# Three-pass query and output projections, and attention copies dealt out anew over ACT and DVE

## The chip, the cores and the metric

The kernel runs on one NeuronCore of a Trainium2 chip. It has five engines with a queue each, which meet only at semaphores: TensorE (PE, matmuls), VectorE (DVE), ScalarE (ACT), GpSimd (POOL) and SyncE (SP, which here issues DMAs). The metric is the device time of one execution in microseconds, lower being better.

## The reference

A gated cross-attention block with a mixture-of-experts feed-forward behind it, all in float32:

```python
# x: (4, 1024, 256), context: (4, 77, 256), 16 heads of 16
q = layernorm(x) @ w_q + b_q;  k = ctx @ w_k + b_k;  v = ctx @ w_v + b_v
attn = softmax(where(mask == 0, -10000, q k^T / 4))          # 1024 x 77 a head
x = x + tanh(g_x) * ((attn v) @ w_o + b_o)
xn = layernorm(x)
routed = top-2 of 4 experts, each silu(xn eg^T) * (xn eu^T) @ ed^T, width 688
shared = silu(xn sg^T) * (xn su^T) @ sd^T
out = x + tanh(g_f) * (routed + shared)
```

## The kernel before

The 4096 rows are cut into 16 units of 256 rows. The first third of the program is a software pipeline of 18 steps, numbered `i` from 0. In step `i` unit `i` has its scores and exponentials; unit `i-1` has its probabilities transposed (`prob_T`, five groups through the one bank `p_t`, each copied to `pT` by `t_copy`) and multiplied by the values (`prob_v`); unit `i-2` has its output projection (`out_proj`), second layernorm (`stats_2`, `rstd2`, `normed_2`), transpose and router logits; unit `i+1` has its transpose (`x_T`) and query projection (`q_T`). From step 4 (`FIRST`) on, the shared expert of earlier units fills TensorE: `gate_up(n, c)` for six chunks `c` of width 128 and `down(n)`. Chunks 0 and 1 and the `down` of the unit before stand in an even step, chunks 2 to 5 in an odd one. After the last step the rest of the shared expert runs along with the routing and the experts' weights, and then come 67 tiles of routed rows. The change touches neither of these later stages.

The order in each engine's queue is written out by hand: a function `step(i)` for each engine calls the pieces in turn. An engine takes its queue strictly in order, so a piece that waits holds all behind it.

Each unit's probabilities come in four quarters `j`: 64 query-by-head blocks of scores on TensorE (`scores(i, j)`), mask and maximum on DVE (`half_max`, a predicated copy and a reduction), eight exponentials with their sums on ACT (`exps`), reciprocals on DVE (`recip`), the scaling on POOL (`normalise`). `scores(i, j)` waits for `exps` two quarters back, since there are two pairs of score banks.

A float32 matmul of this kernel shows as two matmul records and runs at a quarter of the float32r rate. Where a product is to be exact enough in float32r, the operands are split into a high and a low part (`hi` written by ACT or DVE as a rounding copy, `lo` as the difference), and the product is taken in three passes, hi·hi, hi·lo and lo·hi (`PASSES`). Before the change the scores, `gate_up`, `down` and the experts go that way, and the query and output projections are plain float32: `xT_copy` on ACT takes the transposed unit from the bank `p_m` to `xT`, `attention_out` on DVE takes the attention result from `p_m` to `oT`.

In what follows exps(0) to exps(3) are a unit's four groups of eight exponentials, and q_hi is ACT's copy of the query result (`qT_hi`), which is followed by `q_lo` on DVE.

## Time and profile before

| | us |
|---|---|
| median of 3 runs (983.92 to 986.4) | 985.76 |
| the profiled execution | 986.65 |
| its span, first to last instruction | 984.8 |
| PE busy in the span | 902.6 (92%) |
| DVE, ACT, POOL busy in the span | 564.2, 487.6, 465.3 |
| PE, ACT busy from 200 to 300 us | 90.99, 86.85 |
| mean granted TensorE clock | 0.968 |

The profiled execution lies 1.85 us above its span and 0.89 above the median. A busy share counts each engine by itself; TensorE's is high throughout, because a matmul is shown until its result has drained. The first scores start at 17 us and the last output projection at 356; then come the rest of the shared expert, the routing and the experts' weights, and from 527 us on the routed tiles. A clock of 1.00 is 2.4 GHz, 0.50 is 1.2 GHz.

### The profile page before, as it was taken

To read this page: it belongs to the slowest core of one execution; us is meant where nothing else is said; L and a number is where in the kernel's file an instruction comes from. 1 tells how busy PE (TensorE), PEld (TensorE's weight loads), DVE (VectorE), ACT (ScalarE), POOL (GpSimd) and SP (SyncE) were. 2 spreads that over 40 slices of the span, in tenths; PEclk is the share of its full clock that TensorE was granted. 3 is DMA by queue.
4 is the path that set the end of the run, shared out by engine and by line. 5 is a ranking of instruction groups with operands and counts; after the bars stand their busy time and mean duration, and the time that the engine had idled before them with its cause. 6 is when DMAs were issued, how large, how long until landed. Compare 5 with 4: busy or idle time off the path is not lost.

```text
span 984.8 us, 21889 instructions
## 1 busy us (share of the span) xinstructions
PE 902.6 (92%) x6491; PEld 801.4 (81%) x6492; DVE 564.2 (57%) x1293; ACT 487.6 (50%) x1820; POOL 465.3 (47%) x639
## 2 busy tenths in 40 slices
PE   6668889989999889899887999999999999999995
PEld 4445768778787688899886999999999999999995
DVE  5675777677776737777653444444444444444442
ACT  3886988888888733356543323223222322222231
POOL 4355475565645532356631444444444444444442
PEclk9787999999999999999998999999999999999998
DMA  5222322132221221323231222222222222222221
GB/s 171 62 69 83 117 69 81 48 106 69 81 80 38 72 86 34 113 71 122 84 108 51 38 37 43 41 36 40 43 37 37 43 43 37 38 43 38 38 41 22
DMA packets 56863, 61.71 MB, mean 63 GB/s; under 512 B 15642, under 2 KB 45183, under 8 KB 56799
## 3 DMA queue, kind: packets, MB, share of 16 engines
q1 hardware_dynamic: 42871, 43.15, 14.0%
q0 software_dynamic: 12864, 17.57, 11.0%
q8 instruction: 31, 0.51, 0.2%
q10 hardware_dynamic: 1064, 0.21, 0.1%
q14 instruction: 33, 0.27, 0.1%
HBM read 34.78 MB, written 25.82 MB: 62 GB/s over the span
## 4 chain that ended last, share of the span: by engine, by line
PE 73%; ACT 9%; issue 6%; DVE 6%; POOL 5%; DMA 1%; ACTq 0%; DVEq 0%; POOLq 0%
PE p_s L315 26%; PE p_t L325 12%; PE p_f L1810 5%; ACT prob L1040 4%; PE p_f L339 4%; PE p_f L1830 4%; PE p_m L1749 3%; PE p_s L1722 3%; PE p_t L1734 2%; PE p_s L1810 2%; PE p_m L1703 2%; PE p_t L329 2%; PE p_m L300 1%; PE p_m L1761 1%; PE p_s L1830 1%
## 5 line engine op out<-in xcount | busy, mean ns | idle before, releaser
L204 POOL DMA_INDIRECT out_rows<-yout,add_at x67 | 107.1, 1599 | 195.5 <-DVE yout L270 195.5
L1040 ACT ACTIVATE prob<-p_s,negmax 128x77 f32<-128x77 f32 x512 | 159.8, 366 | 3.0 <-DVE negmax L1327 2.8
L277 DVE TENSOR_TENSOR hid<-p_s,sil 128x688 f32<-128x688 f32 x67 | 58.6, 875 | 165.7 <-ACT sil L242 165.7
L242 ACT ACTIVATE sil<-p_s 128x688 f32<-128x688 f32 x67 | 49.9, 745 | 194.2 <-PE p_s L315 194.2
L1040 ACT ACTIVATION_READ_ACCUMULATOR prob<-p_s,negmax 128x1 f32 x512 | 126.5, 249 | 0.0
L315 PE MATMUL p_s<-wgu_hi,fxT_hi 128*128 x402 | 111.4, 385 | 2.2 <-DVE wd_lo L1383 2.2
L315 PE MATMUL p_s<-wgu_lo,fxT_hi 128*128 x402 | 105.7, 371 | 0.0
L315 PE MATMUL p_s<-wgu_hi,fxT_lo 128*128 x402 | 105.1, 370 | 0.0
L247 ACT ACTIVATE hT_hi<-p_f 128x512 fp32r<-128x512 f32 x67 | 40.1, 598 | 125.0 <-PE p_f L339 125.0
L325 PE MATMUL p_t<-wd_hi,hT_hi 128*128 x335 | 99.3, 296 | 2.3 <-DVE hT_hi L290 2.3
L827 POOL TENSOR_TENSOR prob<-prob,rinv 128x616 f32<-128x616 f32 x64 | 77.8, 1217 | 45.9 <-DVE rinv L1334 45.9
L325 PE MATMUL p_t<-wd_hi,hT_lo 128*128 x335 | 94.3, 282 | 0.0
L325 PE MATMUL p_t<-wd_lo,hT_hi 128*128 x335 | 94.1, 281 | 0.0
L188 POOL DMA_INDIRECT xin<-xn_scratch,get_at x67 | 67.7, 1010 | 55.5 <-POOL get_at L185 51.6
L315 PEld LDWEIGHTS p_s<-wgu_hi,fxT_lo 128*128 128x128 f32 x402 | 72.5, 189 | 11.5
L315 PEld LDWEIGHTS p_s<-wgu_lo,fxT_hi 128*128 128x128 f32 x402 | 72.3, 189 | 11.2
L846 POOL TENSOR_TENSOR shT_lo<-shid,shT_hi 128x256 fp32r<-128x256 f32 x80 | 59.1, 750 | 47.0 <-ACT shT_hi L1080 47.0
L286 DVE TENSOR_TENSOR hT_lo<-p_f,hT_hi 128x512 fp32r<-128x512 f32 x67 | 46.4, 692 | 59.3 <-ACT hT_hi L248 59.3
L1810 PE MATMUL p_f<-xnT_hi,swgu_hi 128*128 128x256 f32 x248 | 75.8, 306 | 2.8 <-POOL xnT_lo L840 2.7
L315 PEld LDWEIGHTS p_s<-wgu_hi,fxT_hi 128*128 128x128 f32 x402 | 69.1, 190 | 11.2 <-issue 2.6
L1810 PE MATMUL p_f<-xnT_lo,swgu_hi 128*128 128x256 f32 x248 | 69.8, 281 | 0.0
L1810 PE MATMUL p_f<-xnT_hi,swgu_lo 128*128 128x256 f32 x248 | 69.7, 281 | 0.0
(252 smaller groups left out, 2464.5 us busy)
## 6 DMA issues: line engine op xcount, KB each, us to landing
xr<-in_x SPq DMA_DIRECT2D x16, 256.0 KB, 2.9
x_scratch<-xr SPq DMA_DIRECT2D x16, 256.0 KB, 2.0
xn_scratch<-xn SPq DMA_DIRECT2D x16, 256.0 KB, 2.1
xt_scratch<-xnT SPq DMA_DIRECT2D x16, 256.0 KB, 2.0
xin<-xt_scratch SPq DMA_DIRECT2D x16, 256.0 KB, 3.8
x1in<-x_scratch SPq DMA_DIRECT2D x16, 256.0 KB, 3.2
out_rows<-syout SPq DMA_DIRECT2D x16, 256.0 KB, 2.5
raw<-in_L_ffn_ed SPq DMA_DIRECT2D x4, 688.0 KB, 4.3
```

The costliest lines, as they stand in the source:

```text
L188: pool.indirect_dma_start(xin[k][:, :], None, xn_d, bass.IndirectOffsetOnAxis(get_at[k][:, :], 0)).then_inc(s_gat[k], 16)
L204: pool.indirect_dma_start(out, bass.IndirectOffsetOnAxis(add_at[k][:, :], 0), yout[k][:, :], None, compute_op=ALU.add).then_inc(s_add, 16)
L242: act.activation(sil[:, :], p_gu[:, 0:FF], ACT.Silu).then_inc(s_sil, 1)
L277: nc.vector.tensor_tensor(hid[:, 0:FF], p_gu[:, FF:2 * FF], sil[:, :], ALU.mult).then_inc(s_hid, 1)
L286: nc.vector.tensor_tensor(hT[1][:, 0:4, :], p_h[0][:, :].rearrange("p (c t) -> p c t", t=P), hT[0][:, 0:4, :], ALU.subtract)
L315: last = nc.tensor.matmul(p_gu[:, g0:g1], fxT[a][:, c, :], wgu[b][:, bass.ds(e * KC + c, 1), g0:g1], start=(c == 0 and q == 0), stop=(c == ...
L325: nc.tensor.matmul(p_y[:, 0:H], hT[a][:, c, :], wd[b][:, bass.ds(e * FC + c, 1), :], start=(c == 0 and q == 0), stop=False)
L827: pool.tensor_tensor(pr_, pr_, rinv[:, t, m * HH:(m + 1) * HH].unsqueeze(2).broadcast_to([P, HH, SK]), ALU.mult).then_inc(s_P, 1)
L846: pool.tensor_tensor(hT[1][:, c, :], hid[:, c, :], hT[0][:, c, :], ALU.subtract).then_inc(s_hlo, 1)
L1040: last = act.activation(prob[n % 2][t][:, m * PW + h * SK:m * PW + (h + 1) * SK], p_s[:, 2 * t + h // 4, col:col + SK], ACT.Exp, bias=negm ...
L1810: last = nc.tensor.matmul(bank[:, j * UT * P:(j + 1) * UT * P], swgu[w][:, k, j * SGU + c * P:j * SGU + (c + 1) * P], xns[x][:, n % 2, k, ...
L1830: nc.tensor.matmul(bank[:, t * H:(t + 1) * H], hT[x][:, c, at], swd[w][:, c, :], start=(c == 0 and q == 0), stop=False)
```

## The change

The query and output projections are made in float32r: `xT`, `oT`, `wq` and `wo` become pairs of a high and a low part, and `q_T` and `out_proj` make three passes, 12 matmuls instead of 4. The high part of `xT` is the former copy on ACT; its low part is a new piece on DVE, `xT_low`. The high part of `oT` is a new piece on ACT, `out_hi`, and the low part on DVE, `out_lo`, stands where `attention_out` stood. The weights are split once, `wq` ahead of the first projection and `wo` in step 0. In exchange the fifth `t_copy` of a unit goes from ACT to DVE (`last_t_copy`), and `normed_2` becomes a two-input instruction with a broadcast bias.

The order is changed as well. `normed(i+2)` stands at the end of every step (before, even steps had two of them, one at their start and one at their end, and odd steps none). The rounding copies `h_hi` of chunks 3 to 5, with their differences on POOL, move from the odd step to the start of the next even one. `gate_up(n, 1)` moves in even steps from after the last scores to between `x_T` and `q_T`; `down` is cut in two halves around the logits and the last `prob_T`; in odd steps chunk 4 is cut in two halves around `xn_T` and the fourth `prob_T`. The splitting of the next unit's `xn` (`xn_hi`, `xn_lo`) moves from the odd step to the even one before it. The transposes of the shared weights spread over steps 0 to 3 (3, 3, 3 and 2 groups; before 6 and 5 over two steps), with one load of weights issued in step 1 instead of ahead of the steps.

```diff
@@ sync
+                if i == 1:
+                    sp.wait_ge(s_wtr, 4)
+                    sp.dma_start(raw[0][:, 0:KC * FF].rearrange("p (c i) -> p c i", i=FF),
+                                 v["sd"].rearrange("(c p) i -> p c i", p=P)).then_inc(s_sraw["d"], 16)
@@ scalar
             def xT_copy(n):
-                act.activation(xT[:, :, :], cols(p_m[:, :]), ACT.Copy).then_inc(s_xTc, 1)
+                act.activation(xT[0][:, :, :], cols(p_m[:, :]), ACT.Copy).then_inc(s_xThi, 1)
+            def out_hi(n):
+                act.wait_ge(s_PV, n + 1)
+                wait(act, s_Wo, n)
+                act.activation(oT[0][:, :, :], cols(p_m[:, :]), ACT.Copy).then_inc(s_oThi, 1)
             def step(i):
+                if has(i - 2):
+                    out_hi(i - 2)
                 if has(i - 1):
                     t_copy(i - 1, 0)
-                if not odd and has(i + 1) and i > 0:
-                    normed(i + 1)
+                if f and not odd and n > 0:
+                    h_hi(n - 1, 3)
+                    h_hi(n - 1, 4)
                 if has(i):
                     exps(i, 0)
...
-                if has(i - 1):
-                    t_copy(i - 1, 4)
                 if f and odd:
-                    h_hi(n, 3)
                     gate(n, 5)
-                    h_hi(n, 4)
...
-                if has(i + 2) and not odd:
+                if has(i + 2):
                     normed(i + 2)
@@ vector
-            def attention_out(n):
-                dve.wait_ge(s_PV, n + 1)
+            def out_lo(n):
+                dve.wait_ge(s_oThi, n + 1)
                 wait(dve, s_Wo, n)
-                nc.vector.tensor_copy(oT[:, :, :], cols(p_m[:, :])).then_inc(s_oT, 1)
+                nc.vector.tensor_tensor(oT[1][:, :, :], cols(p_m[:, :]), oT[0][:, :, :], ALU.subtract).then_inc(s_oTlo, 1)
+            def xT_low(n):
+                dve.wait_ge(s_xThi, n + 1)
+                wait(dve, s_q, n)
+                nc.vector.tensor_tensor(xT[1][:, :, :], cols(p_m[:, :]), xT[0][:, :, :], ALU.subtract).then_inc(s_xTlo, 1)
+            def last_t_copy(n):
+                dve.wait_ge(s_T, 5 * n + 5)
+                dve.wait_ge(s_Tc, 5 * n + 4)
+                wait(dve, s_PV, n)
+                nc.vector.tensor_copy(pT[:, 8:10, :], cols(p_t[:, :])).then_inc(s_Tc, 1)
             def normed_2(n):
-                    last = nc.vector.tensor_scalar(xn[:, par, t, :], xr[:, n % XR, t, :], rs[1][:, par, t:t + 1],
-                                                   nb[1][:, par, t:t + 1], ALU.mult, ALU.add)
+                    last = nc.vector.scalar_tensor_tensor(
+                        out=xn[:, par, t, :], in0=xr[:, n % XR, t, :], scalar=rs[1][:, par, t:t + 1],
+                        in1=nb[1][:, par, t:t + 1].broadcast_to([P, H]), op0=ALU.mult, op1=ALU.add)
@@ tensor
             def q_T(n):
-                pe.wait_ge(s_xTc, n + 1)
+                pe.wait_ge(s_xTlo, n + 1)
...
-                        last = nc.tensor.matmul(p_m[:, m * UT * P:(m + 1) * UT * P], wq[:, k, m * P:(m + 1) * P],
-                                                xT[:, k, :], start=(k == 0), stop=(k == KC - 1))
+                        for q, (w, x) in enumerate(PASSES):
+                            last = nc.tensor.matmul(p_m[:, m * UT * P:(m + 1) * UT * P], wq[w][:, k, m * P:(m + 1) * P],
+                                                    xT[x][:, k, :], start=(k == 0 and q == 0),
+                                                    stop=(k == KC - 1 and q == 2))
             def out_proj(n):
-                pe.wait_ge(s_oT, n + 1)
+                pe.wait_ge(s_oTlo, n + 1)
```

ACT's queue at the turn from an odd step to an even one, before. `lg` is the router's logits, `pT` a `t_copy`, `shT_hi` an `h_hi`, `th` a `gate`, `prob` a group of exponentials, `xnT_hi` the `xn_hi`, `xh` a `normed`:

```order
L1059 ACTIVATE lg<-p_m 128x8
L1049 ACTIVATE pT<-p_t 128x512
L1080 ACTIVATE shT_hi<-shid 128x256
L1071 ACTIVATE th<-p_f 48x256
L1080 ACTIVATE shT_hi<-shid 128x256
L1040 ACTIVATE prob_70,rowsum<-p_s,negmax 128x77 x8
L1065 ACTIVATE xnT_hi<-xin 128x512
L1080 ACTIVATE shT_hi<-shid 48x256
L1049 ACTIVATE pT<-p_t 128x512
L1014 ACTIVATE xh<-xr,nb_131,rs_129 128x256 x2
L1040 ACTIVATE prob_67,rowsum<-p_s,negmax 128x77 x8
```

The same turn of the change, from exps(2)'s second half on (`oT_hi` is `out_hi`):

```order
L1054 ACTIVATE prob_72,rowsum<-p_s,negmax 128x77 x4
L1090 ACTIVATE th<-p_f 48x256
L1054 ACTIVATE prob_73,rowsum<-p_s,negmax 128x77 x8
L1028 ACTIVATE xh<-xr,nb_137,rs_135 128x256 x2
L1068 ACTIVATE oT_hi<-p_m 128x512
L1063 ACTIVATE pT<-p_t 128x512
L1099 ACTIVATE shT_hi<-shid 128x256 x2
L1054 ACTIVATE prob_70,rowsum<-p_s,negmax 128x77 x8
```

Between exps(2) and exps(3) a `t_copy` and two `h_hi` have gone; between exps(3) and the next exps(0) `out_hi` has come in, behind `xh`.

DVE's queue from the fourth maximum of an odd step to the first maximum of the next, before (`th` and `shid` are `inner`, `BN_STATS` and `BN_AGGR` are `stats_1`, `blind` is the mask):

```order
L1327 TENSOR_REDUCE negmax<-p_s 128x8
L1344 SCALAR_TENSOR_TENSOR th<-th,p_f 128x256
L1349 TENSOR_TENSOR shid<-p_f,th 128x256
L1259 BN_STATS bst_125<-xr 128x6 x2
L1264 BN_AGGR mv_127<-bst_125 128x2 x2
L1334 RECIPROCAL rinv<-rowsum 128x8
L1344 SCALAR_TENSOR_TENSOR th<-th,p_f 48x256
L1349 TENSOR_TENSOR shid<-p_f,th 48x256
L1312 TENSOR_SCALAR blind<-mask_in 128x154
L1283 COPY oT<-p_m 128x512
L1323 COPY_PREDICATED p_s<-blind,hidden 128x2x308
L1327 TENSOR_REDUCE negmax<-p_s 128x8
```

The same of the change:

```order
L1370 TENSOR_REDUCE negmax<-p_s 128x8
L1325 COPY pT<-p_t 128x512
L1387 SCALAR_TENSOR_TENSOR th<-th,p_f 128x256
L1392 TENSOR_TENSOR shid<-p_f,th 128x256
L1290 BN_STATS bst_131<-xr 128x6 x2
L1295 BN_AGGR mv_133<-bst_131 128x2 x2
L1377 RECIPROCAL rinv<-rowsum 128x8
L1387 SCALAR_TENSOR_TENSOR th<-th,p_f 48x256
L1392 TENSOR_TENSOR shid<-p_f,th 48x256
L1355 TENSOR_SCALAR blind<-mask_in 128x154
L1314 TENSOR_TENSOR oT_lo<-p_m,oT_hi 128x512
L1366 COPY_PREDICATED p_s<-blind,hidden 128x2x308
```

A copy to `pT` has come in behind the fourth maximum, and what stands ahead of the next step's first maximum now reads `oT_hi`, which ACT writes.

## Rows read from the trace of the kernel before

**Rows 1.** Windows exps(0) to exps(0): length, busy PE, PEld, DVE, ACT, POOL, clock, DMA

```profile
100.57:118.26 17.69, 14.65 (x130) 11.80 (x130) 14.04 (x31) 15.97 (x79) 7.70 (x13) 1.00 0.34 107
...
241.04:261.90 20.86, 19.37 (x155) 15.74 (x153) 15.29 (x36) 18.72 (x88) 14.20 (x20) 0.92 0.30 88
...
sum 220.95, PE 202.35 PEld 169.04 DVE 166.05 ACT 189.06 POOL 126.97; mean PE 18.40 PEld 15.37 DVE 15.10 ACT 17.19 POOL 11.54
```

**Rows 2.** Timeline of ACT, odd step 11: start, duration, instruction, idle before

```profile
241.04 0.33 ACT L1040 ACTIVATE prob<-p_s,negmax 128x77 f32<-128x77 f32 x1 [0.28 <-DVE negmax L1327]
...
248.00 0.92 ACT L1027 ACTIVATE qT_hi<-p_m,bq 128x256 fp32r<-128x256 f32 x2
...
252.00 0.33 ACT L1040 ACTIVATE prob<-p_s,negmax 128x77 f32<-128x77 f32 x1
...
254.40 0.23 ACT L1059 ACTIVATE lg<-p_m 128x8 f32<-128x8 f32 x1
254.46 0.66 ACT L1049 ACTIVATE pT<-p_t 128x512 f32<-128x512 f32 x1
254.94 0.49 ACT L1080 ACTIVATE shT_hi<-shid 128x256 fp32r<-128x256 f32 x1
255.25 0.40 ACT L1071 ACTIVATE th<-p_f 48x256 f32<-48x256 f32 x1
...
255.82 0.35 ACT L1040 ACTIVATE prob<-p_s,negmax 128x77 f32<-128x77 f32 x1
```

**Rows 3.** Timeline of ACT, even step 12: exps(0), q_hi, exps(2), exps(3), next exps(0)

```profile
261.90 0.31 ACT L1040 ACTIVATE prob<-p_s,negmax 128x77 f32<-128x77 f32 x1
...
267.93 0.96 ACT L1027 ACTIVATE qT_hi<-p_m,bq 128x256 fp32r<-128x256 f32 x2
...
271.95 0.33 ACT L1040 ACTIVATE prob<-p_s,negmax 128x77 f32<-128x77 f32 x1
...
274.89 0.40 ACT L1040 ACTIVATE prob<-p_s,negmax 128x77 f32<-128x77 f32 x1
...
281.62 0.33 ACT L1040 ACTIVATE prob<-p_s,negmax 128x77 f32<-128x77 f32 x1 [0.28 <-DVE negmax L1327]
```

**Rows 4.** Timeline of PE in step 11: query projection, scores after it, chunk 4, last wait

```profile
245.41 1.89 PE L1703 MATMUL p_m<-xT,wq 128*128 128x256 f32 x8
247.14 0.60 PE L1734 MATMUL p_t<-ident,prob 128*128 128x128 f32 x4
...
248.87 0.39 PE L1810 MATMUL p_f<-xnT_hi,swgu_hi 128*128 128x256 f32 x1
...
250.40 0.60 PE L1772 MATMUL p_m<-ident,xn 128*128 128x128 f32 x4
...
255.18 3.53 PE L1749 MATMUL p_m<-pT,vblk 128*32 128x256 f32 x32 [1.24 <-ACT pT L1049]
```

**Rows 5.** Windows, the value product at the end of step 11, columns as in the first group

```profile
255.10:258.70 3.60, 3.52 (x34) 1.52 (x34) 0.99 (x3) 3.60 (x21) 3.44 (x7) 0.54 0.09 13
```

**Rows 6.** Timeline of DVE, step 11: oT copy, fourth maximum, stats_1; POOL's end of rstd1

```profile
238.57 0.69 DVE L1283 COPY oT<-p_m 128x512 f32<-128x512 f32 x1 [1.14 <-PE p_m L1749]
...
252.25 0.80 DVE L1327 TENSOR_REDUCE negmax<-p_s 128x8 f32<-128x616 f32 x1
...
254.64 0.25 DVE L1264 BATCH_NORM_AGGREGATE mv<-bst 128x2 f32<-128x6 f32 x2
...
256.15 0.60 POOL L808 TENSOR_TENSOR nb<-nb,rs 128x2 f32<-128x2 f32 x1
```

**Rows 7.** The instructions of normed_2: duration in ns, least, median, most

```profile
L1291 DVE TENSOR_SCALAR xn<-xr,rs,nb x32: 401/600/1287, 64.9 to 361.0; 128x256 f32<-128x256 f32 x32
```

**Rows 8.** Timeline ahead of step 0: DVE key blocks, first q_lo; ACT normed(1)

```profile
13.59 2.53 DVE L1386 TENSOR_TENSOR kblk_hi<-kT_hi,own 128x616 fp32r<-128x616 f32 x2
16.41 0.88 DVE L1305 SCALAR_TENSOR_TENSOR qT_lo<-p_m,bq,qT_hi 128x256 fp32r<-128x256 f32 x2 [0.29 <-ACT qT_hi L1027]
...
20.02 1.09 ACT L1014 ACTIVATE xh<-xr,nb,rs 128x256 f32<-128x256 f32 x2 [3.39 <-POOL nb L808]
```

More of the change, by code:

```diff
@@ L918, in step @@
                 odd = (i - FIRST) % 2
-                if i == 1:
+                if i == 2:
                     down_tail()
+                if i > FIRST and not odd:
+                    h_lo(n - 1, 3)
                 if has(i + 1):
@@ L929, in step @@
                     h_lo(n, 1)
+                if i > FIRST and not odd:
+                    h_lo(n - 1, 4)
                 if has(i):
@@ L955, in _ @@
                 step(i)
+            for c in range(3, FC - 1):
+                h_lo(LATE - 1, c)
             route_consts()
@@ L1151, in step @@
                     h_hi(n, 1)
+                if f and not odd and n > 0:
+                    h_hi(n - 1, 5)
                 if has(i):
                     exps(i, 1, 0, HH // 2)
-                if f and odd:
-                    gate(n, 3)
+                if f:
+                    gate(n, 3 if odd else 1)
                 if has(i):
@@ L1196, in _ @@
                 step(i)
+            for c in range(3, FC):
+                h_hi(LATE - 1, c)
             def weigh():
@@ L1444, in step @@
                     stats_2(i - 2)
+                if has(i + 1):
+                    xT_low(i + 1)
                 if f:
@@ L1463, in step @@
                     half_max(i, 3)
-                for w in weights_in(i)[2:4]:
+                for w in weights_in(i)[1:2]:
                     w_lo(w)
-                if f:
-                    inner(n, 4 if odd else 1)
+                if has(i - 1):
+                    last_t_copy(i - 1)
+                if f and odd:
+                    inner(n, 4)
                 if has(i + 2):
@@ L1951, in step @@
                     scores(i, 3)
-                filler(f.get("C"))
-                for w in weights_in(i)[2:4]:
+                between, last_fill = f.get("C"), f.get("D")
+                if between is None and last_fill is not None:
+                    between = last_fill
+                if between is not last_fill:
+                    filler(between, 0)
+                for w in weights_in(i)[1:2]:
                     w_T(w)
+                odd = (i - FIRST) % 2
+                if has(i - 1) and not odd:
+                    prob_T(i - 1, 3)
                 if has(i - 2):
                     xn_T(i - 2)
-                if has(i - 1):
+                if has(i - 1) and odd:
                     prob_T(i - 1, 3)
+                filler(between, int(between is not last_fill))
                 if has(i - 2):
@@ L1962, in step @@
                     prob_T(i - 1, 4)
-                filler(f.get("D"))
-                for w in weights_in(i)[4:]:
+                filler(last_fill, 1 if between is last_fill else None)
+                for w in weights_in(i)[2:]:
                     w_T(w)
```

172 lines of the change are left out of this document (101 added, 71 removed).

## Prediction

> **What bounds the kernel now.** I read the busy shares first. In the attention steps TensorE and ACT are both near full, so neither share decides. I therefore cut the trace where ACT begins exps(0) of each step. The eleven stretches sum to 220.95 us, TensorE busy 202.35 and ACT 189.06 [rows 1]. The first of them, step 4, takes 17.69, as no `down` is ready yet. From 118.26 to 321.52 lie ten steps, or five pairs of an odd and an even one, 40.65 a pair.
>
> Then I follow ACT through a pair. In odd step 11 it goes from exps(0) to q_hi in 6.96 us (241.04 to 248.00), to exps(2) in 4.00, to exps(3) in 3.82, and to the next exps(0) in 6.08 (255.82 to 261.90) [rows 2, 3]. Even step 12 has 6.03, 4.02, 2.94 and 6.73 [rows 3]. The first and third stretches of the odd step are ACT's own work: eight exponentials take 2.40 (252.00 to 254.40), and `pT`, `h_hi` and `gate` 0.48, 0.31 and about 0.3 each [rows 2]. The reader is to see that the step is a loop through ACT, DVE and TensorE in which ACT idles only where it crosses to another engine, above all between exps(3) and exps(0).
>
> At that crossing TensorE decides today. It waits 1.24 for the fifth `t_copy`, and the value product then takes 3.53 [rows 4]. The granted clock there is 0.54, near the lower level, 1.2 GHz [rows 5]. DVE's `oT` copy and first maximum stand behind it: from the start of that copy to the next exps(0) pass 2.47 (238.57 to 241.04) [rows 6, 2].
>
> **The change part by part.** Three passes: the four float32 matmuls of a projection take 1.73 (245.41 to 247.14); 12 float32r ones of the same width take 1.53 with their start (248.87 to 250.40) [rows 4]. So 0.2 is saved at each of 32 projections, 6.4 in all, if TensorE sets the pace. The splitting adds three DVE or ACT pieces a unit of the size of the `oT` copy, 0.69 [rows 6]: `out_hi`, which takes the place of a `t_copy` on ACT, `xT_low`, and on DVE the last copy.
>
> The crossing after the change: exps(3) 2.40, `normed` about 1.0 [rows 8], `out_hi` 0.66 to its end with the handover, and then `out_lo` and the first maximum, which is the stretch of 2.47 above. That is 6.5 in every step. The value product no longer matters, since it can end before `normed` does. Odd to even was 6.08 (5.4 in two steps where the product was fast, 6.1 in three), even to odd 6.73. The sum of the two goes from 12.5 to 13.0. What was gained by an early product is lost because DVE's first maximum now stands behind a copy that stands behind ACT.
>
> The other stretches. Odd, exps(0) to q_hi: the same pieces, 6.96. `xT_low` makes the query projection end later, but ACT comes to q_hi only after exps(1). I make out about 0.8 of room: `stats_2` ends some 3.6 behind exps(0), `xT_low` 0.7 later, the projection at 5.9. Even: one `h_hi` and one `gate` more, 6.64. From q_hi to exps(2): in odd steps it runs over chunk 4, 3.94; in even steps chunk 1 is out of the way and DVE's third maximum decides, 3.5. From exps(2) to exps(3): odd 2.8, since the copy and two `h_hi` (1.1) are gone; even 3.0. The pair is 6.96 + 3.94 + 2.8 + 6.5 + 6.64 + 3.5 + 3.0 + 6.5 = 39.8.
>
> One wait is new. `normed` stands at the end of odd steps too, and needs `stats_1`, which stands behind the last copy. In step 11 the fourth maximum ended at 253.05, `stats_1` at 254.89, POOL's last of `rstd1` at 256.75 [rows 6]. With 0.7 more ahead of it, that is 257.5, or 9.5 behind q_hi, where ACT arrives at 3.94 + 2.8 + 2.4 = 9.1. In even steps the copy waits for the last `prob_T`, with about the same end. I take 0.25 a step, between 0 and 0.5. The pair becomes 40.3, a gain of 0.35, and 1.8 over the five. Queued behind that `normed` is `out_hi`, so the wait is paid in full.
>
> Step 4 loses: it had a crossing of only 4.7 without `down`, and gets one of 6.5; in all 17.69 becomes 19.6, a loss of 1.9.
>
> Ahead of step 0: DVE ends the key blocks at 16.12 and does q_lo at 16.41 [rows 8]. Now `wq_lo`, `xT_low` (1.4 together), the projection (1.6) and q_hi (0.9) lie between, so q_lo starts at about 20.1, and with it everything is 3.6 later. No other work hides it. If the clock is at its lower level there, 1.4 more.
>
> Steps 0 to 3, before from 21.0 to 100.57: fewer weight groups in steps 0 and 1, and no second `normed` ahead of exps(0). By the same pieces they are 17.2, 19.0, 19.3 and 19.4 instead of 79.5 in all, a gain of 4.6. The load moved in SP's queue waits for four transposed groups, which now come early in step 1, and the group that reads it comes in step 2; I cost it at nothing. Should it land late, the third weight group of step 2 slips, which has a step of room.
>
> Steps 15 to 17: the odd step's 1.0 between exps(2) and exps(3), two projections' 0.2 each, less 0.7 for `out_hi` ahead of `out_lo` where nothing covers it; I take 1.1 gained.
>
> `normed_2`: its instructions had a median of 600 ns, from 401 to 1287 [rows 7]. The new form has two inputs like `oT`'s difference. The Trainium skill, "VectorE: DVE Perf Modes", section on the perf-mode tiers, gives a one-input operation on float32 in SBUF twice the rate of a two-input one; by that rule the new form would be some 0.13 us longer each, an estimate from that page. The long ones in the trace say that something holds the old form up, which the rule leaves out. Either way it ends before q_hi does, and the sum holds nothing for it. Nearest rows for the new form: 0.4 to 0.5, a gain of up to 0.4 a step on DVE if it were late, and a loss of 0.3 at most.
>
> Sum: +3.6 - 4.6 + 1.9 - 1.8 - 1.1 = -2.0, of which the clock's absence from the value product is part. The span goes from 984.8 to 982.8, the profiled time from 986.65 to 984.7. The median lay 0.9 below the profiled time, so 983.8; I say 983.7.
>
> **The rivals.** *TensorE sets the pace* (faster). For it: TensorE is the busiest engine, and the waits ahead of the value product, with its half clock, vanish. Then an odd step saves 0.4 by the projections, 1.24 by the wait and 1.0 on average by the clock (1.7 in three of five), an even one 0.4: 3.0 a pair, 15 over five pairs, and with the first steps as above the time is 971. Against it: ACT's own pieces in a pair are some 34 of 40.65, and the crossing of 6.5 does not shorten with TensorE. It needs the start of exps(0) to come within about 5 of exps(3).
>
> *The clock falls at the crossing* (slower). At the step's start TensorE now waits twice: the second scores for exps(3), and `out_proj` for `out_lo`, some 2 us of idle in 4. Before, a wait of 1.24 with transposes and small products ahead of it went with 0.54 [rows 4, 5]. If the clock falls there, `out_proj` and the next chunk take 3.1 more between them; ACT's `gate` behind exps(0) has 1.3 to spare and stalls about 1.5. Slower by over 0.3% begins at 5 / 1.5, about four steps; in eight of the twelve, with the first projection at half clock, it is 997, in six 993. Against it: in two of five odd steps a gap just as long left the clock full, and the stretch after the crossing is dense.
> The Trainium skill, "TensorE: Matmul & The Clock Gate", says that the slow clock is the default and activity lifts it, and that transposes do not count as activity; by it this rival gains, and [rows 5] agrees.
>
> *DVE's queue becomes the loop* (slower). It is busy 15.29 a step [rows 1], and 1.4 come on. If `xT_low` comes over 0.8 late, q_hi follows one for one; 0.5 a step over 12 is 990. Against it: 16.7 of 20 leaves room, and `normed_2` may get shorter.
>
> **How the numbers follow.** Within 0.3% (2.96 us) a measurement of this kernel can't tell from no change. The forecast has 0.57: its own range is 978 to 988, as each of five terms may be off by 1 or 2. It lies 1 us inside the bound, so 0.38 of it is "same", 0.17 faster and 0.02 slower. TensorE's pace 0.21, the clock 0.15, DVE's queue 0.07. Faster 0.38, same 0.39, slower 0.23. The range from 971 to 993 leaves out less than 2 in 10.
>
> **What would show it.** ACT's time from exps(3) to exps(0): 6.5 in odd and even steps alike. From exps(2) to exps(3) in odd steps 2.8. First scores at about 21 instead of 17.3. Exps(0) of step 4 at about 99.6, of step 15 at about 321. The projections at 1.45 to 1.55. The wait ahead of the value product gone, and TensorE idle ahead of `out_proj`. The clock in windows over the steps: 1.00 confirms, 0.9 in most of them is the second rival. The prediction is wrong if pairs take under 39 or over 41.5.

## The result, and the profile after

| | before | after |
|---|---|---|
| median | 986.08 us (983.92 to 987.51, 4 executions) | 995.61 us (991.11 to 998.48, 4 executions) |
| the profiled execution, its span | 986.65, 984.8 | 991.11, 989.2 |
| exps(0) of step 0, 5, 15 | 21.02, 118.26, 321.52 | 26.95, 122.66, 327.42 |

The ratio is 1.0094, with a 95% interval of 1.005 to 1.0138: the changed kernel is slower, by about 1%. A second set of six executions gave 993.55 and 1.0081 (1.0054 to 1.0107). The prediction of 983.7 was 12 too low, and its range ended at 993.

The windows of the profile after, cut where ACT begins exps(0) as in [rows 1]: step 4, odd step 11, even step 12, and the sum over steps 4 to 14. Columns: length, then busy time of PE, PEld, DVE, ACT and POOL, granted clock, share and rate of DMA.

```profile
103.32:122.66 19.34, 16.85 (x139) 13.43 (x139) 14.59 (x34) 16.60 (x79) 9.76 (x14) 0.82 0.44 139
...
245.58:266.14 20.56, 17.31 (x154) 14.55 (x154) 16.51 (x38) 17.96 (x85) 11.91 (x17) 0.95 0.29 87
266.14:287.26 21.12, 19.92 (x182) 17.62 (x181) 16.17 (x36) 17.19 (x80) 11.58 (x16) 0.97 0.21 63
...
sum 224.10, PE 199.82 PEld 170.99 DVE 177.33 ACT 190.60 POOL 131.48; mean PE 18.17 PEld 15.54 DVE 16.12 ACT 17.33 POOL 11.95
```

The sum was 220.95. TensorE is busy a little less than before (199.82 for 202.35), ACT as much, and DVE 1 us a step more (16.12 for 15.10). No engine is full, so the waits must tell.

The timeline of ACT in step 11 and over its end, which answers to [rows 2]: exps(0), q_hi, exps(2), exps(3), `normed`, `out_hi`, `t_copy` 0, the two `h_hi`, and exps(0) of step 12.

```profile
245.58 0.33 ACT L1054 ACTIVATE prob<-p_s,negmax 128x77 f32<-128x77 f32 x1 [1.07 <-DVE negmax L1370]
...
252.48 0.97 ACT L1041 ACTIVATE qT_hi<-p_m,bq 128x256 fp32r<-128x256 f32 x2
...
256.84 0.32 ACT L1054 ACTIVATE prob<-p_s,negmax 128x77 f32<-128x77 f32 x1
...
259.56 0.34 ACT L1054 ACTIVATE prob<-p_s,negmax 128x77 f32<-128x77 f32 x1
...
262.21 1.10 ACT L1028 ACTIVATE xh<-xr,nb,rs 128x256 f32<-128x256 f32 x2
263.21 0.57 ACT L1068 ACTIVATE oT_hi<-p_m 128x512 fp32r<-128x512 f32 x1
263.69 0.58 ACT L1063 ACTIVATE pT<-p_t 128x512 f32<-128x512 f32 x1
264.16 0.71 ACT L1099 ACTIVATE shT_hi<-shid 128x256 fp32r<-128x256 f32 x2
266.14 0.33 ACT L1054 ACTIVATE prob<-p_s,negmax 128x77 f32<-128x77 f32 x1 [1.27 <-DVE negmax L1370]
```

The bracket behind a row is the idle time ahead of it and what ended it. ACT now waits 1.07 and 1.27 for DVE's first maximum, where it waited 0.28. The timeline of DVE shows why.

```profile
263.81 0.69 DVE L1314 TENSOR_TENSOR oT_lo<-p_m,oT_hi 128x512 fp32r<-128x512 f32 x1 [2.46 <-ACT oT_hi L1068]
264.42 0.85 DVE L1366 COPY_PREDICATED_SCALAR p_s<-blind,hidden 128x616 f32 x1
265.31 0.80 DVE L1370 TENSOR_REDUCE negmax<-p_s 128x8 f32<-128x616 f32 x1
266.03 0.19 DVE L1377 RECIPROCAL rinv<-rowsum 128x8 f32<-128x8 f32 x1
267.53 0.75 DVE L1308 SCALAR_TENSOR_TENSOR xr<-p_m,tgx,xr 128x512 f32<-128x512 f32 x1 [1.31 <-PE p_m L1820]
```

DVE idles 2.46 for `out_hi`, which stands on ACT behind `normed`. The scores of which it then takes the maximum were there long before, as TensorE's timeline of the same place shows: scores 0, scores 1, the output projection, and the chunk behind it.

```profile
260.45 0.41 PE L1780 MATMUL p_s<-kblk_hi,qT_hi 64*128 64x308 f32 x2
...
262.16 0.41 PE L1780 MATMUL p_s<-kblk_hi,qT_hi 64*128 64x308 f32 x2 [1.02 <-ACT prob L1054]
...
264.56 0.58 PE L1820 MATMUL p_m<-wo_hi,oT_hi 128*128 128x256 f32 x1 [1.12 <-DVE oT_lo L1314]
264.94 0.42 PE L1820 MATMUL p_m<-wo_lo,oT_hi 128*128 128x256 f32 x1
...
267.29 0.33 PE L1852 MATMUL p_f<-xnT_hi,swgu_hi 128*128 128x256 f32 x1
```

Scores 0 begin at 260.45 and take 0.7, so the maximum could have begun at about 261.2; it did at 264.42. The projection takes 2.73 from its first row to the chunk's. The window over it has the clock at 0.50, its lower level:

```profile
264.50:267.30 2.80, 2.74 (x13) 2.74 (x14) 1.68 (x4) 1.53 (x10) 1.00 (x1) 0.50 0.34 86
```

Of the eleven steps from 4 to 14, this fall of the clock came at the start of steps 8 and 12. At the start of steps 6, 10 and 14 TensorE waited the same 1.12 or 1.13 for `out_lo`, and the projection went at full clock and took 1.52.

### The profile page after: what moved, and what is told of

It is laid out like the page before. It is cut to its first block, busy times and chain, and to the rows that moved or that the text cites. A ratio compares the mean times of both kernels' runs of the same rounds, so it can differ in the third digit from the quotient of the medians.

```text
span 989.2 us, 22212 instructions
## 1 busy us (share of the span) xinstructions
PE 893.8 (90%) x6619; PEld 802.3 (81%) x6620; DVE 583.0 (59%) x1327; ACT 489.9 (50%) x1822; POOL 468.3 (47%) x639
## 3 DMA queue, kind: packets, MB, share of 16 engines
q0 software_dynamic: 12864, 17.57, 11.1%
## 4 chain that ended last, share of the span: by engine, by line
PE 67%; ACT 11%; DVE 10%; issue 7%; POOL 3%; DMA 1%; DVEq 0%; ACTq 0%; POOLq 0%
PE p_s L315 25%; PE p_t L325 12%; ACT prob L1054 6%; PE p_f L339 4%; PE p_f L1897 4%; PE p_f L1852 3%; PE p_s L1852 2%; PE p_t L1792 2%; PE p_t L329 2%; DVE p_s L1366 2%; PE p_m L1807 2%; PE p_m L300 1%; PE p_m L1820 1%; PE p_m L1760 1%; PE p_s L1780 1%
## 5 line engine op out<-in xcount | busy, mean ns | idle before, releaser
L1054 ACT ACTIVATE prob<-p_s,negmax 128x77 f32<-128x77 f32 x512 | 160.4, 361 | 17.3 <-DVE negmax L1370 17.2
L1054 ACT ACTIVATION_READ_ACCUMULATOR prob<-p_s,negmax 128x1 f32 x512 | 124.4, 244 | 0.0
```

Source lines behind the costliest of these rows:

```text
L1054: last = act.activation(prob[n % 2][t][:, m * PW + h * SK:m * PW + (h + 1) * SK], p_s[:, 2 * t + h // 4, col:col + SK], ACT.Exp, bias=negm ...
```

## The experiments

Thirteen edited kernels, and the changed kernel once more. All times are medians, each against executions of the kernel before on the same chip (their medians lie between 985.3 and 987.4). The table holds ACT's stretches of a late undisturbed pair, as the prediction cuts them: exps(0) to q_hi, to exps(2), to exps(3), and across to the next exps(0). "Cross" is that last one. It was read from ACT's timeline of each profile.

| kernel | us | ratio | odd: q_hi, exps(2), exps(3), cross | even: the same | pair |
|---|---|---|---|---|---|
| before | 986.1 | | 6.95, 4.01, 3.82, 6.0 (5.4 in two) | 6.03, 4.03, 2.94, 6.73 | 40.65 (mean) |
| after | 993.6, 995.6 | 1.0081, 1.0094 | 6.91, 4.36, 2.71, 6.58 | 6.60, 3.62, 2.99, 6.65 | 40.42 |
| passes_alone | 1003.4 | 1.0173 | 6.91, 4.03, 3.81, 6.22 | 6.03, 4.38, 2.93, 7.22 | 41.53 |
| order_alone | 970.7 | 0.9829 | 6.96, 4.24, 2.72, 5.02 | 6.59, 3.83, 2.99, 5.88 | 38.22 |
| q_passes | 972.2 | 0.9837 | 6.96, 4.33, 2.72, 5.03 | 6.60, 4.09, 3.00, 5.87 | 38.60 |
| max_first | 1002.3 | 1.0155 | 8.45, 4.33, 2.72, 5.21 | 7.30, 4.27, 2.99, 5.87 | 41.14 |
| hi_early | 982.5 | 0.9953 | 6.91, 4.36, 2.72, 5.39 | 6.60, 3.62, 2.99, 6.38 | 38.97 |
| dve_hi | 980.8 | 0.9942 | 6.91, 4.36, 2.72, 5.02 | 6.58, 3.78, 2.99, 6.45 | 38.80 |
| fill_first | 997.4 | 1.0099 | 6.95, 4.67, 2.72, 6.58 | 6.60, 3.63, 2.99, 6.66 | 40.80 |
| filled | 1004.6 | 1.0178 | 8.82, 4.67, 2.72, 5.02 | 7.57, 4.30, 2.99, 5.87 | 41.97 |
| order_act_copy | 974.9 | 0.9908 | 6.95, 4.24, 3.20, 5.02 (6.3 in three) | 6.59, 3.75, 3.49, 5.38 | 38.62 |
| old_normed_2 | 990.9 | 1.004 | 6.92, 4.11, 2.72, 6.58 | 6.61, 3.43, 2.99, 6.67 | 40.03 |
| order_old_normed_2 | 968.9 | 0.9795 | 6.96, 4.08, 2.72, 5.03 | 6.59, 3.50, 3.00, 5.87 | 37.75 |

prologue (990.7, ratio 1.0043) and dve_hi_prologue (977.6, 0.9905) change nothing in the pairs.

**after_again.** No edit. 

> The changed kernel once more, unedited, to see how its executions scatter: 991.1 to 998.5 in four so far, against 983.9 to 987.5 of the kernel before. Theory A (the crossing: DVE's first maximum stands behind oT_lo, which stands behind ACT's oT_hi, in every step) gives no scatter of its own. Theory B (the clock falls in some of the crossings): each fall costs some 1 to 1.5 us, so a slower execution shows a lower mean clock, and the median is 993 to 997 again, with another execution of 991 possible.

Measured 993.55 (991.88 to 997.14). In steps 5 to 14 of its profile the clock fell at the start of step 12 alone; the odd steps from 5 to 13 all took 20.56 to 20.58, and the even ones but step 12 took 19.58 to 19.89. The mean clock of its six executions runs from 0.973 to 0.961, and the two longest, 995.28 and 997.14, have the lowest, 0.966 and 0.961, though 993.85 has the highest. The kernel before scatters in the same way: 982.72 at 0.976, 990.48 at 0.961. So falls of the clock go with much of the scatter of either kernel, and they do not make the 40.42, which is a pair at full clock.

The clock fell at another place as well, in step 0. There TensorE multiplies the context by its value weights (`wv`), first in the profile after and then in this one:

```profile
24.32 3.68 PE L1979 MATMUL p_f<-wv,ctxT 128*77 128x256 f32 x16
24.00:26.00 2.00, 2.00 (x14) 1.34 (x11) 1.62 (x7) 0.04 (x1) 1.32 (x7) 1.00 0.00 0
```
```profile
25.33 5.62 PE L1979 MATMUL p_f<-wv,ctxT 128*77 128x256 f32 x16
24.00:26.00 2.00, 2.00 (x14) 1.52 (x11) 1.65 (x6) 0.00 (x0) 1.12 (x4) 0.50 0.00 0
```

At half clock the product is 1.94 longer. Exps(1) comes 6.15 behind exps(0) instead of 3.42, and step 0 takes 20.77 instead of 18.46. In all the thirteen edited kernels' profiles this product took 4.32 to 5.82, in order_alone too (5.17); the profiles before and after, with 3.68, are the only two in which all of it ran at full clock.

**order_alone.** The order of the change without its passes; the fifth copy stays on DVE, and `normed_2` keeps its new form:

```diff
-                if has(i - 2):
-                    out_hi(i - 2)
                 if has(i - 1):
                     t_copy(i - 1, 0)
...
             def out_lo(n):
-                dve.wait_ge(s_oThi, n + 1)
+                dve.wait_ge(s_PV, n + 1)
...
-                nc.vector.tensor_tensor(oT[1][:, :, :], cols(p_m[:, :]), oT[0][:, :, :], ALU.subtract).then_inc(s_oTlo, 1)
+                nc.vector.tensor_copy(oT[:, :, :], cols(p_m[:, :])).then_inc(s_oTlo, 1)
...
-                if has(i + 1):
-                    xT_low(i + 1)
```

and the projections as they were. 

> The changed kernel's order on all engines, but with the projections of before: plain float32 operands, xT by ACT's copy alone, oT by one copy on DVE that waits for the value product alone; no oT_hi, no lo parts. Theory A: the crossing loses the handover and falls to 4.7 to 5.3, the prologue is back at 21, and the time is 966 to 978. Theory B alone (a long idle stretch of TensorE at the crossing whatever stands in it): the wait for exps(3) stays, falls go on in some steps, 980 to 986. If the order itself is what costs, 988 or more.

Measured 970.7, ratio 0.9829 (0.9797 to 0.9861). The order alone gains 15.5, of which the fifth copy's place on DVE is about 4 (order_act_copy, below). The crossing is 5.02 and 5.88 instead of 6.58 and 6.65, and everything else in the pair is within about 0.2 of after. The timeline of DVE ahead of its step 12, to be held against that of after above:

```profile
244.33 0.69 DVE L1296 COPY oT<-p_m 128x512 f32<-128x512 f32 x1
244.94 0.85 DVE L1344 COPY_PREDICATED_SCALAR p_s<-blind,hidden 128x616 f32 x1
245.83 0.80 DVE L1348 TENSOR_REDUCE negmax<-p_s 128x8 f32<-128x616 f32 x1
```

ACT ends `normed` there at 246.25 and begins exps(0) at 247.54 without a wait for the maximum. The crossing is ACT's own work again.

**passes_alone.** The other half: the kernel before with the three passes, `out_hi` at ACT's step start, and `wq_lo` and `xT_low(0)` ahead of the key products:

```diff
+                if has(i - 2):
+                    out_hi(i - 2)
                 if has(i - 1):
                     t_copy(i - 1, 0)
...
                 if has(i - 2):
                     stats_2(i - 2)
+                if has(i + 1):
+                    xT_low(i + 1)
```

> The kernel before, in its own order, with the projections in three passes and nothing else of the change: oT_hi by ACT at the step's start, oT_lo on DVE in the place of the oT copy, xT_lo behind stats_2, wq_lo and xT_lo(0) ahead of the key products, the fifth copy of pT still on ACT, normed_2 in its old form. The order alone gave 970.7. If the passes cost by the handover at the crossing (oT_hi 0.57 ahead of oT_lo, and behind ACT's fifth copy), each step gets 0.6 to 1.2 longer, 986.2 + 8 to 14 + about 2 for the prologue = 996 to 1002. Rival: TensorE's shorter projections pay for it, 984 to 990.

Measured 1003.4, ratio 1.0173 (1.0149 to 1.0197). The odd step's crossing grows from 6.0 to 6.2, the even step's from 6.73 to 7.22, and in even steps q_hi to exps(2) grows by 0.35. The five pairs hold only 5.6 of the loss (208.81 for 203.26). The start is 2.4 later, steps 0 to 4 are 2.3 longer, and what follows the start of step 15 is 4.6 longer, by the one profile of each; for that last part no run shows the cause. The two halves sum to 17.1 - 15.5 = +1.6. The changed kernel with the same prologue edit measured +4.4 (prologue, below), so the halves add up to within 3.

**max_first.** On DVE:

```diff
-                if has(i - 2):
-                    out_lo(i - 2)
                 if has(i):
                     half_max(i, 0)
+                if has(i - 2):
+                    out_lo(i - 2)
```

> On DVE the first maximum stands ahead of oT_lo. Nothing else moves. Theory A: in step 12 of the profile after, ACT waits 1.27 for that maximum (odd steps about 2), though its scores were there 3 us before; the wait goes, the crossing from exps(3) to exps(0) falls from 6.6 to about 5.3 ahead of even steps and 4.7 ahead of odd ones, and if TensorE does not take over, some 1.3 to 1.9 are gained in each of 14 steps: 972 to 980. Theory B: the idle time of TensorE ahead of out_proj stays, the clock falls as often, so less than half of this arrives: 985 to 991. Theory C (TensorE's own work is the bound already): under 4 us gained, 992 or more.

Measured 1002.3, ratio 1.0155 (1.0125 to 1.0186). My theory was half of the truth. The crossing fell to 5.2 and 5.9 as it said. But exps(1) came 1.5 later in odd steps, and the pair got 0.7 longer. DVE and TensorE in its step 11:

```profile
250.37 0.68 DVE L1314 TENSOR_TENSOR oT_lo<-p_m,oT_hi 128x512 fp32r<-128x512 f32 x1
250.97 0.19 DVE L1377 RECIPROCAL rinv<-rowsum 128x8 f32<-128x8 f32 x1
252.83 0.75 DVE L1308 SCALAR_TENSOR_TENSOR xr<-p_m,tgx,xr 128x512 f32<-128x512 f32 x1 [1.67 <-PE p_m L1820]
253.50 0.85 DVE L1366 COPY_PREDICATED_SCALAR p_s<-blind,hidden 128x616 f32 x1
254.39 0.80 DVE L1370 TENSOR_REDUCE negmax<-p_s 128x8 f32<-128x616 f32 x1
```
```profile
251.11 0.39 PE L1820 MATMUL p_m<-wo_hi,oT_hi 128*128 128x256 f32 x1 [1.53 <-DVE oT_lo L1314]
```

`out_lo` is at the head of two chains. One is the first maximum and exps(0). The other is the output projection, `attended`, the second maximum and exps(1), since `half_max(i, 1)` stands behind `attended` in DVE's queue. Whichever of the two is put first, the other pays. So the handover itself must come earlier.

**hi_early.** That is what this does, on ACT:

```diff
-                if has(i - 2):
-                    out_hi(i - 2)
                 if has(i - 1):
                     t_copy(i - 1, 0)
...
                 if has(i):
                     exps(i, 3)
+                if has(i - 1):
+                    out_hi(i - 1)
                 if has(i + 2):
                     normed(i + 2)
```

> The changed kernel with ACT's oT_hi moved from the start of the next step to just behind exps(3), ahead of normed. The value product has ended 1.4 before exps(3) does, so oT_hi need not wait. Theory A': what costs is the chain oT_hi, oT_lo, out_proj, attended, second maximum, together with oT_lo, first maximum; both begin 1.25 earlier (normed's 1.0 and its wait), normed itself comes 0.5 later. The crossing falls from 6.6 to 5.3 to 5.6 in each step, and exps(1) does not slip: 0.9 to 1.2 in 14 steps, 977 to 982. Rival: TensorE's own work is next at once (it is busy 17.8 of 20), 986 to 990.

Measured 982.5, ratio 0.9953 (0.9932 to 0.9974), 11 less than after_again. The odd crossing falls by 1.2, the even one by only 0.3: there `down` keeps TensorE busy to the value product, and ACT waits for that before `out_hi`. Exps(1) does not slip.

**dve_hi.** Both parts on DVE:

```diff
             def out_lo(n):
-                dve.wait_ge(s_oThi, n + 1)
+                dve.wait_ge(s_PV, n + 1)
                 wait(dve, s_Wo, n)
+                nc.vector.tensor_copy(oT[0][:, :, :], cols(p_m[:, :])).then_inc(s_oThi, 1)
+                dve.wait_ge(s_oThi, n + 1)
```

and no `out_hi` on ACT. 

> The changed kernel with both parts of oT on DVE: a copy to float32r and the difference right behind it, as soon as the value product has ended; ACT has no oT_hi. DVE idles 2.5 at that place (261.35 to 263.81 in step 12), so both parts end some 2.5 earlier than now, TensorE need not wait ahead of out_proj, and the first maximum is done before ACT ends normed. Theory A': the crossing is then ACT's own work, 4.3 to 5.0, the pair falls from 40.4 to 37 to 38.5: 970 to 980. Rival: DVE, 16.0 busy of 20 and now 0.7 more, or TensorE at 18.9 of 20 as in order_alone, takes over: 980 to 988.

Measured 980.8, ratio 0.9942 (0.9923 to 0.9961). The odd crossing is 5.02, the same as with no split at all. The even one is 6.45, 0.57 above order_alone, by the one more instruction on DVE:

```profile
234.49 0.69 DVE L1312 CAST oT_hi<-p_m 128x512 fp32r<-128x512 f32 x1 [1.14 <-PE p_m L1807]
235.21 0.69 DVE L1314 TENSOR_TENSOR oT_lo<-p_m,oT_hi 128x512 fp32r<-128x512 f32 x1
235.82 0.85 DVE L1366 COPY_PREDICATED_SCALAR p_s<-blind,hidden 128x616 f32 x1
236.71 0.80 DVE L1370 TENSOR_REDUCE negmax<-p_s 128x8 f32<-128x616 f32 x1
```

**prologue.** On DVE, ahead of the steps:

```diff
+            dve.wait_ge(s_wphi, 1)
+            nc.vector.tensor_tensor(wq[1][:, :, :], wq_raw[:, :, :], wq[0][:, :, :], ALU.subtract).then_inc(s_wplo, 1)
+            xT_low(0)
             for m in range(KC):
                 key_hi(m)
-            dve.wait_ge(s_wphi, 1)
-            nc.vector.tensor_tensor(wq[1][:, :, :], wq_raw[:, :, :], wq[0][:, :, :], ALU.subtract).then_inc(s_wplo, 1)
-            xT_low(0)
```

> On DVE, ahead of the steps, wq_lo and xT_low(0) stand ahead of the two key products, no longer behind them; nothing else moves. If the 5.9 us by which exps(0) of step 0 is late come from the chain wq_lo, xT_low, q_T at half clock, q_hi, q_lo, then the two products (about 2 us with their waits) come out of it, and wq_lo, which took 1.70 beside POOL's work, may take less: exps(0) of step 0 at 23 to 25 instead of 26.95, and 990 to 993 in all. Rival: ACT's wq_hi (behind kT) is what is late; then wq_lo cannot start earlier and the gain is under 1 us.

Measured 990.7, ratio 1.0043 (1.0023 to 1.0064), 2.9 less than after_again, and exps(0) of step 0 at 23.41 instead of 26.95. DVE and TensorE in the profile after, then DVE with this edit:

```profile
16.09 1.70 DVE L1456 TENSOR_TENSOR wq_lo<-wq_raw,wq_hi 128x512 fp32r<-128x512 f32 x1
17.71 0.68 DVE L1319 TENSOR_TENSOR xT_lo<-p_m,xT_hi 128x512 fp32r<-128x512 f32 x1
22.35 0.88 DVE L1348 SCALAR_TENSOR_TENSOR qT_lo<-p_m,bq,qT_hi 128x256 fp32r<-128x256 f32 x2 [3.96 <-ACT qT_hi L1041]
```
```profile
18.45 0.58 PE L1760 MATMUL p_m<-xT_hi,wq_hi 128*128 128x256 f32 x1 [6.45 <-DVE xT_lo L1319]
...
23.28 0.41 PE L1780 MATMUL p_s<-kblk_hi,qT_hi 64*128 64x308 f32 x2 [1.60 <-DVE qT_lo L1348]
```
```profile
13.57 0.68 DVE L1454 TENSOR_TENSOR wq_lo<-wq_raw,wq_hi 128x512 fp32r<-128x512 f32 x1
14.17 0.69 DVE L1319 TENSOR_TENSOR xT_lo<-p_m,xT_hi 128x512 fp32r<-128x512 f32 x1
```

**dve_hi_prologue.** Both edits. 

> dve_hi together with the edit of prologue (wq_lo and xT_lo(0) ahead of the key products). The two touch different stretches, so their gains should add: dve_hi less 3, with exps(0) of step 0 at about 23.4. Where both theories hold this is the fastest with three passes, 967 to 977; order_alone stands at 970.7.

Measured 977.6, ratio 0.9905 (0.9882 to 0.9928): against after_again the two edits gained 12.8 and 2.9 by themselves, and 15.9 together. It is the fastest with all operands split.

**fill_first.** On TensorE, a test of the clock's falls at the crossing:

```diff
+                filler(f.get("A"))
                 if has(i - 2):
                     out_proj(i - 2)
                 if i == 0:
                     values_of_context()
-                filler(f.get("A"))
```

> The changed kernel with TensorE's first chunk of gate and up products (1.42) ahead of the output projection instead of behind it, so that the wait of 1.1 for oT_lo is filled. Nothing else moves. Theory B (falls of the clock at the crossing are what costs): steps such as 12, in which the projection went at half clock after that wait, are gone, the executions scatter less and the median falls by 2 to 4, to 990 to 992, with a mean clock of 0.97 or more. Theory A' (the handovers ahead of the first maximum and of the projection are what costs, with the clock at full level in nearly all pairs): the wait ahead of the first maximum is as before, the pair stays at 40.4, only step 12 gains 1.2: 992 to 995.

Measured 997.4, ratio 1.0099 (1.0073 to 1.0126). With the wait filled, nine windows of 20 us from 130 to 310 all show a clock of 1.00, and the kernel is no faster. The odd step is 0.35 longer, in the stretch ahead of exps(2), since the projection and all that hangs on it come later; over five pairs that is 1.8, about as much as falls of the clock had cost. The even step stays at 19.86. So the clock at the crossing is not the main loss.

**q_passes.** order_alone with the query projection in three passes and the prologue edit:

```diff
             def q_T(n):
-                pe.wait_ge(s_xThi, n + 1)
+                pe.wait_ge(s_xTlo, n + 1)
...
+                if has(i + 1):
+                    xT_low(i + 1)
```

> order_alone (970.7) with three passes in the query projection alone, and wq_lo and xT_lo(0) ahead of the key products; the output projection and oT as in order_alone. If only the splitting of oT costs in the steps, and xT_lo has room behind stats_2, the pairs stay at 38.2 or get up to 0.2 shorter, and the prologue costs 2.2 to 2.4: 971 to 973.5. Rival: xT_lo's 0.7 comes too late for the query projection or pushes DVE's queue, 0.3 or more a step: 976 or more.

Measured 972.2, ratio 0.9837 (0.9812 to 0.9863), 1.5 above order_alone, which is inside the scatter of order_alone (965.1 to 971.3). By the profiles the start is 1.3 later (22.54 against 21.21), and a pair is 0.4 longer, nearly all in DVE's stretch ahead of exps(2), behind `xT_low`. The crossing is as in order_alone, 5.03 and 5.87. So it is the output side whose splitting costs at the crossing, and in time: with the prologue edit, splitting `oT` as well gives 977.6 with both parts on DVE, and 990.7 with `out_hi` on ACT.

**filled.** dve_hi_prologue with the edits of max_first and fill_first. 

> dve_hi_prologue (977.6) with two edits more: on DVE the first maximum ahead of both parts of oT, and on TensorE the first chunk ahead of the output projection. In max_first the first edit alone shortened the crossing to 5.2 and 5.9 but made oT_lo 1.5 later, and with it the projection, attended and exps(1). Here the chunk covers that time on TensorE, and oT_hi does not wait for ACT. If TensorE's idle time is what bounds the pair of 38.8, it falls to 38.0 and the time to 971 to 975. Rival: attended, still late, holds DVE's second maximum back as in max_first, exps(1) slips by 0.5 to 1.5 a step: 982 to 995.

Measured 1004.6, ratio 1.0178 (1.0152 to 1.0204). The rival held: `attended` is late, exps(1) comes at 6.16 instead of 4.25 behind exps(0), and it costs more than the 0.6 that the even crossing gains.

**order_act_copy.** order_alone with the fifth copy on ACT:

```diff
+                if has(i - 1):
+                    t_copy(i - 1, 4)
...
-                if has(i - 1):
-                    last_t_copy(i - 1)
```

> order_alone (970.7) with the fifth copy of pT back on ACT, behind lg_copy and ahead of exps(3), instead of on DVE. In order_alone ACT is busy 17.6 of 20 and waits little between exps(0) and exps(3), so this 0.48 lies on its path: exps(2) to exps(3) goes from 2.72 and 2.99 to about 3.2 and 3.5, and the step gets 0.3 to 0.5 longer, in 15 steps: 975 to 979, about half of what the order gained. Rival: TensorE, full ahead of odd steps, covers it, or DVE is relieved by the same amount: 970 to 973.

Measured 974.9, ratio 0.9908 (0.9882 to 0.9934), 4 above order_alone. The stretch ahead of exps(3) is 0.5 longer in both steps, and the even step's crossing is 0.5 shorter. TensorE again waits for ACT's copy ahead of the value product, 1.48 or 1.49 in each of the five odd steps. In steps 7 and 11 the product went at full clock all the same, and the crossing is 5.02. In the other three it went at half clock, and the crossing is 1.3 longer. The timeline of both cases (steps 11 and 9) and the window over the second:

```profile
249.18 1.93 PE L1772 MATMUL p_m<-pT,vblk 128*32 128x256 f32 x32 [1.48 <-ACT pT L1056]
...
209.25 3.60 PE L1772 MATMUL p_m<-pT,vblk 128*32 128x256 f32 x32 [1.49 <-ACT pT L1056]
```
```profile
209.00:213.00 4.00, 3.75 (x34) 1.61 (x36) 1.06 (x4) 3.82 (x20) 3.84 (x7) 0.57 0.36 78
```

That is [rows 4, 5] once more, and with the copy on DVE it is gone.

**old_normed_2** and **order_old_normed_2.** The line of `normed_2` as it was, in the changed kernel and in order_alone:

```diff
-                    last = nc.vector.scalar_tensor_tensor(
-                        out=xn[:, par, t, :], in0=xr[:, n % XR, t, :], scalar=rs[1][:, par, t:t + 1],
-                        in1=nb[1][:, par, t:t + 1].broadcast_to([P, H]), op0=ALU.mult, op1=ALU.add)
+                    last = nc.vector.tensor_scalar(xn[:, par, t, :], xr[:, n % XR, t, :], rs[1][:, par, t:t + 1],
+                                                   nb[1][:, par, t:t + 1], ALU.mult, ALU.add)
```

> The changed kernel with normed_2 in its old form (one input and two scalars instead of two inputs). The two instructions took 1.43 together in step 11 of the profile after, and 1.15 in passes_alone, which has the old form. If DVE's queue sets the stretch from q_hi to exps(2) in odd steps (normed_2, q_lo and the third maximum stand in a row there, and the scores are ready before them), that stretch falls from 4.36 to about 4.1 and the pair from 40.42 to 40.15, 1.5 over the run of pairs and up to 3 in all: 991 to 993.5. Rival: the old form is held up by something beside it, as its longest instruction of 1287 ns suggests, and wins nothing: 4.36 stays.

> order_alone (970.7) with normed_2 in its old form. The same reading: 4.24 in odd steps becomes 4.0, even steps (3.74 to 3.83) change by 0.0 to 0.2, so 968 to 970.5. Rival: 4.24 stays and with it 970.7.

Measured 990.9 (1.0023 to 1.0057 of before, 12 executions), 2.6 less than after_again, and 968.9, ratio 0.9795 (0.9764 to 0.9826), the fastest of all. The time against order_alone, 1.8, is inside the scatter. The stretches are not. Ahead of exps(2) the changed kernel has 0.25 less in odd steps and 0.19 in even ones, and order_alone has 0.16 and about 0.26. DVE after and with the old form:

```profile
252.32 1.43 DVE L1333 SCALAR_TENSOR_TENSOR xn<-xr,rs,nb 128x256 f32<-128x256 f32 x2
253.67 0.19 DVE L1377 RECIPROCAL rinv<-rowsum 128x8 f32<-128x8 f32 x1
253.79 0.82 DVE L1348 SCALAR_TENSOR_TENSOR qT_lo<-p_m,bq,qT_hi 128x256 fp32r<-128x256 f32 x2
254.53 0.85 DVE L1366 COPY_PREDICATED_SCALAR p_s<-blind,hidden 128x616 f32 x1
```
```profile
254.22 1.14 DVE L1333 TENSOR_SCALAR xn<-xr,rs,nb 128x256 f32<-128x256 f32 x2
```

## Why the prediction was wrong

The crossing was right. The prediction added its parts to 6.5 in every step, and 6.6 was measured. Its reason, that the first maximum stands behind a copy that stands behind ACT, is shown by order_alone (5.02 where that is not so), by hi_early and by dve_hi. What it left out is that the output projection, `attended` and the second maximum hang on the same copy. That changes no number of the forecast, and max_first shows that it decides which repair works.

The undisturbed pair came at 40.42 for a forecast of 40.3, and that is partly luck. The 0.25 a step for the wait of `normed` is not there: in step 11 exps(3) ends at 262.11 and `normed` begins at 262.21, in order_alone with the same gap of 0.1. POOL's last of `rstd1` ended at 262.18, 9.7 behind q_hi, and ACT came at 9.6 and not at 9.1, since the stretch ahead of exps(2) was longer than forecast. The missing wait of 0.5 a pair and that stretch, 0.54 a pair, nearly cancel.

The forecast for the profiled execution was 984.7, and it took 991.1. The 6.4 between them are:

- **Ahead of step 0**, +2.3. The step that failed: `wq_lo` and `xT_low` at 1.4 together, and the clock's 1.4 left out. `wq_lo` took 1.70 instead of 0.7, beside POOL, and TensorE, idle for 6.45, ran the projection at a clock of 0.50 (18.45 to about 21.3). The start was 5.9 late instead of 3.6. With the order of prologue, step 0 begins 3.5 earlier.
- **Steps 0 to 4**, +1.2. I had forecast 2.7 gained, and 1.5 were (95.71 against 97.24). The five steps took 18.46, 19.44, 19.15, 19.32 and 19.34 for forecasts of 17.2, 19.0, 19.3, 19.4 and 19.6, so the term that was too small is step 0, by 1.3, and step 1 by 0.4. In step 0 the stretch from exps(2) to exps(3) got 0.7 shorter, and the one from exps(0) to q_hi 0.35 longer, where TensorE now waits 1.55 for `xT_low`. I had also left out the clock in step 0. Here its fall came late and cost little: the query projection from 30.98 took 2.16 instead of 1.53.
- **The pairs**, +3.3. 204.76 instead of 203.26, where I had forecast 1.8 less. Two falls of the clock at a crossing, in steps 8 and 12, cost 1.2 each. A first odd step of 20.96 costs 0.4. The rest, about 0.4, is the stretch from q_hi to exps(2), 4.36 and 3.62 for a forecast of 3.94 and 3.5, less the wait for `normed` that did not come. The step that failed is "it ends before q_hi does, and the sum holds nothing for it": `normed_2` ends after q_hi has begun (253.7 against 252.48), DVE's q_lo and third maximum stand behind it (TensorE began their scores at 251.81), and its new form costs 0.25 there.
- **Steps 15 on**, -0.4: 661.8 against 663.3, 1.5 gained where I forecast 1.1.

Then the median. I had put it 0.9 below the profiled execution, as before. It lay 4.5 above in the first set; over all ten executions of the changed kernel it is about 994.1, 3 above. The profiled one was the fastest of the ten, and its context product in step 0 was spared the half clock, which cost the other profiled execution 2.3 and is found, for part of that product at least, in the profile of every edited kernel. The step that failed here is "The median lay 0.9 below the profiled time": it took over the distance that the kernel before had. The longest executions show a lower mean clock still, and none of those was traced, so the rest of the 4.5 stays open.

**The rivals.** *The clock falls at the crossing* (0.15) happened as a mechanism, with the idle time, the half clock and the stall of ACT as described, at 1.2 a time instead of 1.5, but in one or two steps of eleven. Its time of 993 was closer than mine, which is luck for the most part: the two falls hold 2.4 of the 12, and the first projection at half clock, which it named too, 1.3. fill_first shows that a kernel without the falls at the crossings is no faster. *TensorE sets the pace* (0.21) said 971, and order_alone, which lacks the handover, takes 970.7. That is chance, since the rival's sum holds 0.4 a step for shorter projections and a start 3.6 later, and order_alone has neither. TensorE is busy 36.00 of 38.23 in a pair of it, and waits little. The saving itself was half of what I had read: at the query side a projection went from 1.73 to 1.53, at the output side from 1.54 (both before, 239.96 to 241.50, and in order_alone) to 1.52. *DVE's queue* (0.07) is real in one stretch, and not as I had it: `xT_low` does not hold q_hi up (6.96 and 6.60 in q_passes as in order_alone). What comes later is the third maximum, by 0.25 for `normed_2` and by 0.1 to 0.3 for `xT_low` (q_passes).

I weighed one rule of the Trainium skill and set it aside: "VectorE: DVE Perf Modes", the section on the perf-mode tiers, by which the two-input form is slower. The pair of instructions took 1.43 instead of 1.14 or 1.15, 0.14 more each, where the estimate from that page was 0.13. The page was right in rule and size, and I was wrong on whether anyone waits.

Of the clock, the rows show a level of 0.50 over the first projection, after TensorE had been idle for 6.45. At the crossings the same wait does not decide it: in step 11 of max_first a wait of 1.53 for `oT_lo` left the projection at full clock (251.11 to 252.63), in step 12 of after waits of 1.02 and 1.12 did not. The Trainium skill, "TensorE: Matmul & The Clock Gate", section "What's actually happening", has the slow clock as the default, and the first projection agrees. What else the prediction took from that page no run here tells apart.

## What to carry to other kernels

A split operand costs little by the time of its two instructions and much by the handover between engines. Where the first part stands on one engine's queue behind something else and the second on another's ahead of something urgent, both queues stall, so put both parts on the engine that has the idle time, or move the first to where its input is ready (here 12.8 and 11.1 us). Before reordering around such a point, list every chain that starts from it: here the maximum and the projection both did. And test the two halves of a change apart. This one held an order worth 1.7% and passes that cost as much. And look at whether the one profiled execution is typical: here it was the fastest of ten, and in step 0 its clock stayed up over a product where the others' fell.
